# A second expert layer that fetches rows by a table of places instead of scattering them

## The reference

```python
def _top2_gating(logits, capacity):
    gates = softmax(logits)                       # [N, 8], N = 1792
    mask1 = one_hot(argmax(gates)); mask2 = one_hot(argmax(gates * (1 - mask1)))
    pos1 = cumsum(mask1, axis=0) - mask1
    mask1 = mask1 * (pos1 < capacity)
    pos2 = cumsum(mask2, axis=0) - mask2 + sum(mask1, axis=0)
    mask2 = mask2 * (pos2 < capacity)
    g1, g2 = sum(gates * mask1), sum(gates * mask2); denom = max(g1 + g2, eps)
    # combine[n, e, c] = g / denom at the place c that token n has with expert e
capacity = ceil(2 * 1.25 * N / 8)                 # 560
expert_in = einsum('nec,nh->ech', combine > 0, x)
hmid = silu(einsum('ech,ehf->ecf', expert_in, w1) + b1)      # 128 -> 512
expert_out = einsum('ecf,efh->ech', hmid, w2) + b2           # 512 -> 128
y = einsum('nec,ech->nh', combine, expert_out)
out = y + 0.1 * (silu(x @ sw1 + sb1) @ sw2 + sb2)            # the shared expert
```

## Time and profile before

| | us |
|---|---|
| median of 3 runs | 1610.15 (1605.52 to 1614.38) |
| profiled execution | 1613.86 |
| its span, first to last instruction | 1611.9 |
| PE busy | 1453.4 (90%) |
| DVE busy | 1037.6 (64%) |
| ACT busy | 827.6 (51%) |
| POOL busy | 672.4 (42%) |
| mean granted clock of PE | 0.95 |

### The profile page before, as it was taken

One profiled execution on the slowest core, in us unless ns is written; L12 is line 12 of the kernel. 1 busy time (PEld: TensorE's weight loads), 2 busy tenths in 40 slices (PEclk: granted clock), 3 DMA queues, 4 the chain that ended last, 5 costly groups with the idle time before them and its releaser, 6 DMA issues. The chain is left out here.

```text
span 1611.9 us, 43113 instructions
## 1 busy us (share of the span) xinstructions
PE 1453.4 (90%) x16061; PEld 1116.6 (69%) x16061; DVE 1037.6 (64%) x1692; ACT 827.6 (51%) x1297; POOL 672.4 (42%) x732
## 2 busy tenths in 40 slices
PE   7988899989999987679999999999999999985684
PEld 4445676679999656357777777777777777764583
DVE  4334545668788559467777777777777777535362
ACT  5553333432222337436666666666666666654461
POOL 2300000477787546444433444334443344147263
PEclk9879999999999999789999999999999999987797
DMA  2064984131110320285556655666556655331402
GB/s 78 23 173 136 241 240 131 40 110 63 65 42 23 55 51 2 61 199 116 129 141 153 136 129 127 143 153 134 129 127 143 153 133 129 83 80 38 110 25 85
DMA packets 72884, 174.36 MB, mean 108 GB/s; under 512 B 14989, under 2 KB 44286, under 8 KB 72800
## 3 DMA queue, kind: packets, MB, share of 16 engines
q1 hardware_dynamic: 67936, 157.72, 40.1%
q10 hardware_dynamic: 2688, 11.78, 2.5%
q0 software_dynamic: 2176, 3.71, 0.7%
HBM read 87.58 MB, written 9.56 MB: 60 GB/s over the span
## 5 line engine op out<-in xcount | busy, mean ns | idle before, releaser
L2006 DVE TENSOR_REDUCE hat_tops<-banks 128x1 f32<-128x500 f32 x672 | 439.3, 676 | 153.1 <-PE banks L1751 153.0
L1879 ACT ACTIVATE hat_pb<-banks 125x896 f32<-125x896 f32 x384 | 340.3, 916 | 226.5 <-PE banks L1770 222.7
L1751 PE MATMUL banks<-hat_kh,hat_qm 128*128 128x500 f32 x672 | 298.1, 462 | 5.7 <-DVE hat_tops L2006 3.5
L1770 PEld LDWEIGHTS banks<-hat_q,hat_k 128*125 128x125 f32 x1536 | 219.8, 189 | 74.8 <-issue 32.4
L1770 PE MATMUL banks<-hat_q,hat_k 128*125 128x224 f32 x1536 | 250.8, 286 | 16.2 <-ACT hat_pb L1879 9.2
L1948 POOL CAST hat_kh<-hat_kf 128x500 fp32r<-128x500 f32 x96 | 58.5, 609 | 404.3 <-ACT hat_kf L1892 388.3
L1761 PE MATMUL banks<-hat_pb,hat_vs 125*27 125x168 f32 (+1 forms) x6144 | 166.9, 261 | 0.1
L1761 PEld LDWEIGHTS banks<-hat_pb,hat_vs 125*27 125x27 f32 (+1 forms) x6144 | 132.2, 98 | 43.9 <-issue 24.4
L1751 PEld LDWEIGHTS banks<-hat_kh,hat_qm 128*128 128x128 f32 x672 | 127.8, 192 | 47.4 <-DVE hat_tops L2006 32.8
L1315 ACT ACTIVATE ffn_rg<-banks 128x448 f32<-128x448 f32 x128 | 69.9, 546 | 166.2 <-PE banks L1248 166.0
L1954 POOL TENSOR_TENSOR hat_kl<-hat_kf,hat_kh 128x500 fp32r<-128x500 f32 x96 | 118.2, 1258 | 2.1 <-DMA hat_k<-hat_kh 2.1
(11 more groups left out here) (338 smaller groups left out, 2721.8 us busy)
## 6 DMA issues: line engine op xcount, KB each, us to landing
hat_k<-hat_kh SPq DMA_DIRECT2D x256, 187.5 KB, 4.8
hat_ct<-ctxT SPq DMA_DIRECT2D x32, 750.0 KB, 6.1
hat_k<-hat_kl SPq DMA_DIRECT2D x128, 187.5 KB, 4.5
ctx_cx<-ctx SPq DMA_DIRECT2D x32, 672.0 KB
ctx_cd<-ctxT ACTq DMA_DIRECT2D x15, 750.0 KB, 5.0
ffn_cb<-expert_weights SPq DMA_DIRECT2D x8, 896.0 KB, 4.4
moe_raw<-Mw SPq DMA_DIRECT2D x18, 256.0 KB, 4.0
ctx_cx<-ctx SPq DMA_DIRECT2D x32, 78.0 KB
```

The costliest lines, as they stand in the source:

```text
L1751: peak_out.inc(nc.tensor.matmul(g.bank(PK + m % 2)[:, 0:SB], qm[u][:].rearrange("p h i -> p (h i)")[:, r * 128:r * 128 + 128], kh[u][:, c ...
L1770: mm = nc.tensor.matmul(g.bank(2 * (t % 2) + j // 2)[0:SW, (j % 2) * QW:(j % 2 + 1) * QW], k3[u][:, j, t * SW:(t + 1) * SW], q3[u][:, j, : ...
L1879: exped.inc(nc.scalar.activation(pb[t % 6][:].rearrange("p (n i) -> p n i", n=2), g.ps[0:SW, 2 * (t % 2):2 * (t % 2) + 2, 0:2 * QW], ACT.E ...
L2006: peaked.inc(v.tensor_reduce(tops[:, r, n:n + 1], g.bank(PK + m % 2)[:, 0:SB], AX_X, ALU.max))
```

## The change

No row is scattered before the experts run. The turned tiles are stored plainly, in token order, into a DRAM tensor `rows` (4 DMAs by SP, from the buffers `back`). Each expert's 560 places are four tiles of 128 and a remainder of 48; the remainders of two experts share a tile, so there are 36 tiles of places. `Dispatch` takes the place of `Route`. TensorE sums the one-hots of each tile (`on_pe_tally`) and, with two constant matrices, gets running counts without a scan on VectorE (`on_pe_places`). `lay_out` turns them into a tile and a lane for each token and choice, and makes two one-hots of them: `tile_of` (28 x 36, times the token's number) and `lanes` (28 x 128). `on_pe_list` adds the 28 products of these, which gives the table: for each lane and tile the number of the token there. `name` makes two integer lists of it. GpSimd fetches an expert's rows from `rows` into SBUF by one list (4 or 5 indirect DMAs, four row buffers) and sends its results to `token_rows` by the other (4 or 5). Three experts are fetched before the first send; the others in turn with the sends.

Around it: logits are made chunk by chunk inside the norm; the remainders of x and of the shared expert's units are all VectorE's; six up parts of the shared expert run before its first down part, and the tally, the places and the list stand among them; `lots` is made by ACT in 28 instructions of 128 elements, four behind each expert; weight sets go from six to four, so that five casts and not three fall beside the experts; `back` has four buffers; the two halves of the splits `eh` and `el` become one instruction each; constants grow by 292 columns.

```diff
-    out["slot_base"] = np.tile(float(CAPACITY) * np.arange(E) - SLOTS, (128, 1))
+    pair, odd = np.arange(E) // 2, np.arange(E) % 2
+    out["slot_base"] = np.tile(128.0 * (9 * pair + 4 * odd - 9 * E // 2), (128, 1))
+    out["rest_base"] = np.tile(512.0 - 448 * odd, (128, 1))
+    out["tile_start"] = np.tile(128.0 * np.arange(9 * E // 2), (128, 1))
+    out["lane"] = np.tile(1.0 * np.arange(128), (128, 1))
     token = np.arange(TT)[None] * 128 + p[:, None]
+    out["token_id"] = np.concatenate([token, NT + token], axis=1) - float(NOWHERE)
+    out["tiles_before"] = np.concatenate([(of_expert[:, None] == of_expert[None, :TT * E]) & (of_tile[:, None] < of_tile[None, :TT * E]),
+                                          of_expert[:, None] == np.arange(E)[None]], axis=1) * 1.0
...
+    def on_pe_tally(self, pe, bank):
         nc = self.g.nc
+        pe.wait_ge(self.taken, 2)
+        for k in range(2):
+            flat = self.hot[:, k].rearrange("p t e -> p (t e)")
+            mm = nc.tensor.matmul(bank[0:TT * E, k * 128:k * 128 + 128], flat, self.g.c["ones"], start=True, stop=True)
+        mm.then_inc(self.summed, 1)
+    def on_act_tally(self, act, bank):
+        act.wait_ge(self.summed, 1)
+        self.g.nc.scalar.copy(self.by_tile[:], bank[0:TT * E, 0:256]).then_inc(self.summed_kept, 1)
+    def on_pe_places(self, pe, bank):
+        nc, c_ = self.g.nc, self.g.c
+        pe.wait_ge(self.summed_kept, 1)
+        for k in range(2):
+            at = k * (TT * E)
+            nc.tensor.matmul(bank[:, at:at + TT * E], c_["before"], self.hot[:, k].rearrange("p t e -> p (t e)"), start=True, stop=False)
+            nc.tensor.matmul(bank[:, at:at + TT * E], self.by_tile[:, k * 128:k * 128 + 128], c_["tiles_before"][0:TT * E, 0:TT * E], start=False, stop=True)
+        for k in range(2):
+            at = 2 * TT * E + k * E
+            mm = nc.tensor.matmul(bank[:, at:at + E], self.by_tile[:, k * 128:k * 128 + 128], c_["tiles_before"][0:TT * E, TT * E:], start=True, stop=True)
+        mm.then_inc(self.placed, 1)
+    def on_pe_list(self, pe, bank):
+        nc = self.g.nc
+        pe.wait_ge(self.tiled, 1)
+        for n in range(2 * TT):
+            if n % 7 == 0:
+                pe.wait_ge(self.laned, n // 7 + 1)
+            mm = nc.tensor.matmul(bank[:, 0:self.tiles], self.lanes[:, n, :], self.tile_of[:, n, :], start=(n == 0), stop=(n == 2 * TT - 1))
+        mm.then_inc(self.listed, 1)
...
+    def lay_out(self, dve, bank, bases):
+        g, v, c_ = self.g, self.g.nc.vector, self.g.c
+        half, both = TT * E, lambda ap: spread(spread(ap, 1, TT), 1, 2)
+        dve.wait_ge(self.placed, 1)
+        places = bank[:, 0:2 * half].rearrange("p (k t e) -> p k t e", k=2, e=E)
+        bases(dve, places, bank[:, 2 * half:2 * half + E], bank[:, 2 * half + E:2 * half + 2 * E])
+        self.step(dve, v.tensor_tensor(self.counts[:], self.pos[:], self.hot[:], ALU.mult))
+        self.step(dve, v.tensor_reduce(self.row[:, 4:6, :], self.counts[:], AX_X, ALU.add))
+        flat = self.row[:, 4:6, :].rearrange("p k t -> p (k t)")
+        self.step(dve, v.tensor_scalar(self.start[:], flat, 128.0 * self.tiles - 63.5, GRAIN, ALU.add, ALU.add))
+        self.step(dve, v.tensor_scalar(self.start[:], self.start[:], GRAIN, None, ALU.subtract))
+        self.step(dve, v.scalar_tensor_tensor(out=self.lane[:], in0=flat, scalar=128.0 * self.tiles, in1=self.start[:], op0=ALU.add, op1=ALU.subtract))
+        self.step(dve, v.tensor_tensor(self.tile_of[:], spread(self.start[:], 2, self.tiles), spread(c_["tile_start"][:, 0:self.tiles], 1, 2 * TT), ALU.is_equal))
+        v.tensor_tensor(self.tile_of[:], self.tile_of[:], spread(c_["token_id"], 2, self.tiles), ALU.mult).then_inc(self.tiled, 1)
+        for n in range(4):
+            part = slice(7 * n, 7 * n + 7)
+            v.tensor_tensor(self.lanes[:, part, :], spread(self.lane[:, part], 2, 128), spread(c_["lane"], 1, 7), ALU.is_equal).then_inc(self.laned, 1)
+    def name(self, dve, bank):
         v = self.g.nc.vector
+        ids = bank[:, 0:self.tiles]
+        dve.wait_ge(self.listed, 1)
+        self.step(dve, v.tensor_scalar(self.second[:], ids, float(NT - NOWHERE), float(NT), ALU.is_ge, ALU.mult))
+        v.scalar_tensor_tensor(out=self.fetch_id[:], in0=ids, scalar=float(NOWHERE), in1=self.second[:], op0=ALU.add, op1=ALU.subtract).then_inc(self.named, 1)
+        v.tensor_scalar(self.send_id[:], ids, float(NOWHERE), None, ALU.add).then_inc(self.named, 1)
...
-                    if s == SETS - 1:
-                        sp.wait_ge(sent_all, 16 * 2 * TT)
-                        for e in range(E):
-                            sp.dma_start(rows[e][:], g.slot_rows[e * CAPACITY:(e + 1) * CAPACITY].rearrange("(n p) c -> p n c", p=PART)).then_inc(rows_in[e], 16)
-                for e in range(E):
-                    sp.wait_ge(out_sent[e], 16 * 5)
+                    if s == RAWS - 1:
+                        for i, (a, b) in enumerate(GROUPS):
+                            sp.wait_ge(rows_kept, i + 1)
+                            sp.dma_start(g.rows[a * 128:b * 128].rearrange("(t p) d -> p t d", p=128), back[i][:, 0, 0:b - a, :]).then_inc(rows_stored, 16)
+                sp.wait_ge(rows_stored, 16 * len(GROUPS))
+                for u in range(2):
+                    sp.wait_ge(out_sent[u], 16 * 4 * E // 2)
+                    sp.wait_ge(rest_sent[u], 16 * E // 4)
...
-                        sp.wait_ge(joined, i - 1)
-                        sp.dma_start(back[i % 2][:, k, 0:b - a, :], source).then_inc(back_in[i % 2], 16)
+                        sp.dma_start(back[i][:, k, 0:b - a, :], source).then_inc(back_in[i], 16)
...
+                for t in (*rows, *rest_rows, *rest_ow):
+                    nc.gpsimd.memset(t[:], 0.0).then_inc(cleared, 1)
+                for s in range(3):
...
-                    nc.gpsimd.tensor_tensor(chunk(xl, c), chunk(g.xn, c), chunk(xh, c).bitcast(F32), ALU.subtract).then_inc(x_low, 1)
-                    nc.gpsimd.tensor_copy(sent[:, 1, a:b, 0:D], sent[:, 0, a:b, 0:D]).then_inc(rows_doubled, 1)
-                    nc.gpsimd.tensor_tensor(ring0(hl, j), ring0(hf, j), ring0(hh, j).bitcast(F32), ALU.subtract).then_inc(low0_pool, 1)
-                for k in range(2):
-                    pool.wait_ge(pick.slotted, k + 1)
-                    for t in range(TT):
-                        nc.gpsimd.indirect_dma_start(out=g.slot_rows, out_offset=bass.IndirectOffsetOnAxis(ap=pick.slot[:, k, t:t + 1], axis=0),
-                                                     in_=sent[:, k, t, :], in_offset=None, bounds_check=SLOTS - 1, oob_is_err=False).then_inc(sent_all, 16)
-                def send(e):
-                    pool.wait_ge(out_kept, e + 1)
-                    for n in range(5):
-                        nc.gpsimd.indirect_dma_start(out=g.token_rows, out_offset=bass.IndirectOffsetOnAxis(ap=rows[e][:, n, D:D + 1].bitcast(mybir.dt.int32), axis=0),
-                                                     in_=ow[e % 2][:, n, :], in_offset=None, bounds_check=2 * NT - 1, oob_is_err=False).then_inc(out_sent[e], 16)
+                def fetch(to, q, signal, n):
+                    nc.gpsimd.indirect_dma_start(out=to, out_offset=None, in_=g.rows, in_offset=bass.IndirectOffsetOnAxis(ap=pick.fetch_id[0:n, q:q + 1], axis=0),
+                                                 bounds_check=NT - 1, oob_is_err=False).then_inc(signal, 16)
+                def fetch_rows(e):
+                    if e >= ROWS:
+                        pool.wait_ge(turned, e - ROWS + 1)
+                    for n in range(4):
+                        fetch(rows[e % ROWS][:, n, :], tile_at(e, n), rows_in[e % ROWS], 128)
+                def fetch_rest(m):
+                    if m >= 2:
+                        pool.wait_ge(turned, 2 * m - 2)
+                    fetch(rest_rows[m % 2][0:64 + REST, :], rest_at(m), rest_in[m % 2], 64 + REST)
+                def send(source, q, signal, n):
+                    nc.gpsimd.indirect_dma_start(out=g.token_rows, out_offset=bass.IndirectOffsetOnAxis(ap=pick.send_id[0:n, q:q + 1], axis=0),
+                                                 in_=source, in_offset=None, bounds_check=2 * NT - 1, oob_is_err=False).then_inc(signal, 16)
+                def send_rows(e):
+                    pool.wait_ge(out_kept, 2 * e + 2)
+                    for n in range(4):
+                        send(ow[e % 2][:, n, :], tile_at(e, n), out_sent[e % 2], 128)
+                pool.wait_ge(rows_stored, 16 * len(GROUPS))
+                pool.wait_ge(cleared, ROWS + 4)
+                pool.wait_ge(pick.named, 2)
+                for e in range(3):
+                    fetch_rows(e)
+                    if e % 2 == 0:
+                        fetch_rest(e // 2)
                 for e in range(E):
-                    send(e)
+                    if e + 3 < E:
+                        fetch_rows(e + 3)
+                        if (e + 3) % 2 == 0:
```

(66 more changed lines are left out.)

265 lines of the change are left out of this document (113 added, 152 removed).

## The result

In one set of runs the changed kernel took 1622.9 us (median of 20, 1605.5 to 1635.1), the kernel before 1606.2 (median of 20, 1601.3 to 1618.2). The ratio is 1.0079, 95% interval 1.0059 to 1.0099: slower by 0.8%, where 1606 was forecast from a kernel then measured at 1610. Four of the 20 executions of the changed kernel, among them the profiled one (1630.6), took over 1.5% more than its fastest and are left out of the ratio.

The account below looks back on a forecast made before the run. GpSimd was to become the bound among the experts. Winning 2.2 at turn 7, less 0.8, plus 1.25 for one send fewer made 2.6; with 1.4 at reading back, 4.0 off 1610.15 gave 1606, range 1595 to 1613.

Parts of the forecast that it names:

- To the list: Last stage up to the table of places: first shared matmul at 1441.9, list of 11.8 us at low clock ending 1469.7.
- Rival (a): List on TensorE: it raises the clock, so list and slow shared parts go faster; 5.7 us more won, 1600; chance 0.27.
- (d): Before turn 0: fetches come too late, needing over 3 us each; ends as (c); chance 0.15 together with (c).
- the 18.5 us for 26 shared parts: Shared expert behind the list: five parts at low clock and 21 at high take 18.5 us, ending at 1488.2.
- Expert 0: Starts 12.2 us earlier, at 1489.0, and takes 19 us to its hand-over instead of 22.1: 1508.0.
- The gap that I took away: TensorE's 24.56 us wait before expert 0: its removal was to let expert 0 no longer start at clock 0.50.
- The price of a fetch: GpSimd's instructions among the experts: quiet 0.94 or 0.97 us plus 0.30 issue, stretched to 1.40 beside a busy VectorE.
- (b): GpSimd's instructions among the experts keep their quiet price, 1.27 us: 4.7 us more won, 1601; chance 0.13.
- (c): VectorE instructions with two SBUF operands hold up GpSimd's descriptors for their full length: 16.3 us later, 1622; 0.15 with (d).
- The experts' pace: GpSimd becomes the bound: 36 instructions of 1.40 us behind expert 0's hand-over, so turn 7 at 1560.5, not 1562.66.
- The wider upper bound, 1613: Top of the forecast range: a mean GpSimd instruction of 1.6 us among the experts, 7.2 us later.
- The end: From turn 7 on: `lots` loses 0.8 us, one send fewer wins 1.25, reading back without its 1.34 gap wins 1.4.

Follow-up runs that it names:

- run 1: The changed kernel again, unaltered, for a second profile and set of times: 1616.4 us against 1607.3 of the kernel before, ratio 1.0072.
- run 3: The changed kernel with its 36 fetches as plain loads from SyncE's queue, leaving out the choice of rows: 1585.3 us, ratio 0.9883 to the kernel before.
- run 4: The kernel before plus 18 fetches by a table that nobody reads, behind the last scatter: 1621.8 us against 1607.3, ratio 1.0091.
- run 5: The kernel before plus 18 scatters by a table to a DRAM tensor nobody reads, behind the last scatter: 1620.3 us against 1608.3, ratio 1.0069.
- run 7: The kernel before plus 8 unread fetches by a table, each issued when the one before has landed: 1622.7 us against 1608.3, ratio 1.0053.
- run 9: The kernel before plus 16 unread fetches by a table, in fours that each wait for the previous four's landing: 1621.1 us against 1607.5, ratio 1.0078.
- run 12: The changed kernel with GpSimd waiting for landings after each early expert's four fetches and behind each expert's sends: 1610.9 us against 1610.5 before, ratio 1.0004.
- run 6: The kernel before plus plain loads of 128 x 520 bytes on GpSimd's queue, without a table, behind the last scatter: 1610.2 us, ratio 1.0019.
- run 8: The changed kernel with its 36 fetches as plain loads on GpSimd's queue, leaving out the choice of rows: 1590.3 us, ratio 0.9889 to the kernel before.
- run 11: The kernel before with the changed kernel's way to the places and shared expert order, old scatters, loads and sends: 1603.0 us against 1607.5, ratio 0.9967.

## Why the prediction was wrong, point by point

**To the list: right.** First shared matmul 16.4 for 16.9; `lay_out` 6.4 us from 1442.05 to 1448.5, predicted 6.2; `lanes` 4.09 for 4.0; list at the low clock (granted 0.50) 12.13 for 11.8. Rival (a) is out. So is (d), as no wait on a DMA stands before turn 0. Run 1 has turn 0 at 61.4 against 64.0, so the 18.5 us for 26 shared parts were even a little long.

**Expert 0: 2 us too short.** I let it take 19 us, since it would start at full clock. In run 3, with no update late there, it took 21.3 from turn to hand-over (1478.60 to 1499.9): TensorE waits 0.81 and 1.75 us around the turn, and the granted clock from 1480 to 1484 is 0.61. The gap that I took away was not the only one.

**The price of a fetch: right.** A quiet one is 1.00 + 0.30, where I had bounded it by 0.97 and 1.94. The first 18 instructions from send 0 took (1540.53 - 1517.05) / 17 = 1.38 a step, predicted 1.40. So (b) and (c) are both out; that (c) had 1622 and the median is 1622.9 is chance. The Trainium skill's rule (SBUF — State Buffer, "Who interferes with whom"), that the later of two contending instructions waits the whole length, would have needed 1.85 by the prediction's own working of (c). Single instructions are stretched to 1.2 to 1.5, the mean is 1.38, and the kernel is slower for another reason.

**The experts' pace: this step failed.** The sum had the shared expert and the experts at their old pace and GpSimd as the one bound, 36 steps behind hand-over 0 (the last fetch starts 35 steps behind send 0, so its own terms give 1560.1 for the rows of turn 7, not 1560.5). What GpSimd's transfers do to TensorE's signals it put at nothing. In run 1 send 0 is at 86.4; 35 steps of 1.37 and a landing of 2.3 would put the rows of turn 7 at 136.7. GpSimd stood idle 6.5 us before send 2, since hand-over 2 was late, so the rows landed at 142.8, and turn 7 came another 6.0 us behind them: 148.8. In the profile shown first, turn 0 was 12.7 us late as well, and turn 7 came at 164.0 for a predicted 135.5. Both delays are TensorE's late signals. Runs 4 and 5 show that table transfers make them, runs 7 and 9 that single ones and fours do not, run 12 that with pauses most of them go, runs 3, 6 and 8 that plain loads do not make them.

**Why no rival had it.** The prediction asked what GpSimd's transfers cost GpSimd, and what VectorE does to them. It took it that they cost TensorE nothing, by the kernel before. But there among the experts the sends go in fives with pauses, and half of the scatters run beside an idle TensorE. No row of before has 18 table transfers beside busy experts, and the prediction, which named GpSimd as without a pause from 1508 to turn 7, did not see that as a condition that no row covered. The wider upper bound, 1613, held only the price of an instruction.

**The end: right.** From turn 7 to the end of the stage 49.2 us before, 47.1 after and 46.5 in run 1. The prediction's parts of it (0.8 lost, 1.25 and 1.34 won) make 1.8 less; 2.2 and 2.7 were measured. The joins run in one piece.

**The size.** Without the fetches' side effects the change is worth 1.2% (run 3), though there the loads also cost GpSimd less. With pauses it is worth nothing (run 12), because the 36 table transfers behind hand-over 0 and their pauses are then the bound; the forecast of a small gain was the case of no pauses and no lateness, which no run with these fetches had.

## What to carry to other kernels

In this kernel, moving a long series of transfers by a table from an idle stretch into a busy one was not free for TensorE even where GpSimd had the time. Look how long the unbroken runs are, cut them with a wait, and count the pause. And when a padding experiment comes out slow, look at where in the trace: runs 7 and 9 came out near the time of one theory and had the trace of the other.

## What the runs showed that was not expected

- Beside runs of 18 transfers by a table, what TensorE signals reached ScalarE up to 12.8 us late (13.7 in run 4); signals of ScalarE and VectorE were not late beside it. The first late ones stand some 9 to 13 us, or 7 to 10 transfers, into a run (runs 1, 4 and 5 and the first profile). In the runs of 26 and 29, made mostly of sends, the "remote" gaps begin 33 and 37 us in.
- It is the signal that is late and not the matmul, though matmul ends are modelled: a later matmul starts at 1481.74, on time for its input, while an earlier one's silu still waits until 1489.19, and six updates come within 0.25 us at 1489.12 to 1489.37.
- Left open: which resource it is; why a long run is not enough by itself: in the kernel before the scatters from 1458.53 on stand beside a TensorE that is busy 14.15 of 19 us (1458 to 1477), and all its recorded updates there are within 0.02 us, while run 11 has three gaps beside the same 28; and whether a plain load is harmless as such or because 18 of them last only 10 us (run 8) or 16 with waits between (run 6). A run of plain loads of 25 us was not tried.
- For some landings of table fetches GpSimd waited 5.4 to 6.9 us beside the first experts and SyncE's loads of all rows (runs 7 and 9), against 2.1 for the last scatter. Why is open.
